# Growth and decay rows of the last tile of pass 1 loaded ahead, in buffers that nothing needs any more

## The reference

```python
q = (x @ Wq.T); k = (x @ Wk.T); v = (x @ Wv.T)            # [S, 16, 64] each
log_decay = -softplus(x @ Wd.T + bd)                      # [S, 16], one a head
k_gated = k * sigmoid(x @ Wg.T)
s_t = exp(g_t) * s_{t-1} + k_t^T v_t                      # state 64 x 64 a head
o_t = q_t s_t
out = rmsnorm(o) * norm_w * sigmoid(x @ Wog.T) @ Wo.T
```

## Time and profile before

| | us |
|---|---|
| three runs | 3225.49, 3229.1, 3230.01; median 3229.1 |
| profiled execution, its own time | 3229.59 |
| its span, first to last instruction | 3227.8 |
| TensorE busy | 3162.5 (98%) |
| VectorE, ScalarE, GpSimd busy | 1881.0, 1292.1, 470.6 |
| mean granted TensorE clock | 0.99 of full |

### The profile page before, as it was taken

One profiled execution on the slowest core, in us unless ns is written; L12 is line 12 of the kernel. 1 busy time (PEld: TensorE's weight loads), 2 busy tenths in 40 slices (PEclk: granted clock), 3 DMA queues, 4 the chain that ended last, 5 costly groups with the idle time before them and its releaser, 6 DMA issues. The chain is left out here.

```text
span 3227.8 us, 91060 instructions
## 1 busy us (share of the span) xinstructions
PE 3162.5 (98%) x37253; PEld 2968.2 (92%) x37253; DVE 1881.0 (58%) x4823; ACT 1292.1 (40%) x3584; POOL 470.6 (15%) x723
## 2 busy tenths in 40 slices
PE   7999999999999999999999979999999999999999
PEld 6999999999999999999999968999999999999998
DVE  5454554545554545555545455667666677767776
ACT  3444444444444444444444442333333333333332
POOL 0111111111111111111111112111111111111110
PEclk8999999999999999999999989999999999999999
DMA  6132222322222232222322243222222333332220
GB/s 216 59 104 73 96 86 69 106 68 97 84 79 96 69 99 81 87 89 71 103 75 92 77 149 95 78 78 78 78 79 82 83 84 81 81 81 79 78 78 27
DMA packets 273394, 279.46 MB, mean 87 GB/s; under 512 B 24720, under 2 KB 221344, under 8 KB 273072
## 3 DMA queue, kind: packets, MB, share of 16 engines
q1 hardware_dynamic: 270960, 270.67, 27.6%
q10 hardware_dynamic: 2112, 4.19, 0.4%
HBM read 189.84 MB, written 84.93 MB: 85 GB/s over the span
## 5 line engine op out<-in xcount | busy, mean ns | idle before, releaser
L55 PE MATMUL psJ<-h_hi,w_k_hi 128*128 128x256 f32 x1024 | 298.9, 292 | 0.0
L55 PE MATMUL psJ<-h_hi,w_q_hi 128*128 128x256 f32 x1024 | 296.2, 289 | 0.0
L55 PE MATMUL psJ<-h_hi,w_g_hi 128*128 128x256 f32 x1024 | 293.1, 286 | 2.7 <-DVE h_lo L883 2.1
L55 PE MATMUL psG<-h_hi,w_og_hi 128*128 128x256 f32 x1024 | 286.4, 280 | 4.1 <-PEq L348 4.1
L56 PE MATMUL psJ<-h_lo,w_q_hi 128*128 128x256 f32 x1024 | 286.6, 280 | 0.0
L56 PE MATMUL psJ<-h_lo,w_g_hi 128*128 128x256 f32 x1024 | 286.4, 280 | 0.0
L57 PE MATMUL psJ<-h_hi,w_g_lo 128*128 128x256 f32 x1024 | 286.4, 280 | 0.0
L57 PE MATMUL psJ<-h_hi,w_q_lo 128*128 128x256 f32 x1024 | 286.2, 279 | 0.2 <-issue 0.2
L56 PE MATMUL psJ<-h_lo,w_k_hi 128*128 128x256 f32 x1024 | 285.3, 279 | 0.0
L57 PE MATMUL psJ<-h_hi,w_k_lo 128*128 128x256 f32 x1024 | 285.3, 279 | 0.0
L56 PE MATMUL psG<-h_lo,w_og_hi 128*128 128x256 f32 x1024 | 283.6, 277 | 0.0
(11 more groups left out here) (264 smaller groups left out, 9404.5 us busy)
## 6 DMA issues: line engine op xcount, KB each, us to landing
grown<-cum_dram SPq DMA_DIRECT2D x256, 128.0 KB
cum_rows<-cum_dram SPq DMA_DIRECT2D x512, 64.0 KB, 3.9
o_dram<-o SPq DMA_DIRECT2D x256, 128.0 KB, 4.5
o_cols<-o_dram SPq DMA_DIRECT2D x128, 256.0 KB, 4.9
an_norm_x<-in_L_attn_x_dram SPq DMA_DIRECT2D x32, 512.0 KB, 3.7
h_dram<-h_hi SPq DMA_DIRECT2D x32, 512.0 KB, 3.6
h_dram<-h_lo SPq DMA_DIRECT2D x32, 512.0 KB, 4.6
h_hi<-h_dram SPq DMA_DIRECT2D x32, 512.0 KB, 3.9
```

The costliest lines, as they stand in the source:

```text
L55: nc.tensor.matmul(out, w_hi, x_hi, start=first, stop=False)
```

## The change

In all tiles: cum_rows now holds eight pairs (both halves of its places are used), with a semaphore for each pair, so decay rows no longer wait for the decays four pairs ahead; and at the end of a tile the growth rows of pairs 0 and 1 are issued first, then the decay rows.

At the end of tile 31 all eight pairs' decay rows are issued, not four. In the last tile the growth rows of pairs 2 and 3 go into gate, those of 4 and 5 into grown and those of 6 and 7 into the first two pairs of q, each once its place is dead; SyncE issues them ahead of and between the loads of jobs 0 and 1. And o of the last tile is made in kg, so copy_o waits for no store.

```diff
-        spread = [ctx.enter_context(nc.semaphore(f"a_spread{n}")) for n in range(4)]
+        spread = [ctx.enter_context(nc.semaphore(f"a_spread{n}")) for n in range(NP)]
+        grow_end = [ctx.enter_context(nc.semaphore(f"a_grow_end{n}")) for n in range(1, ND)]
+        grown_end = [grown, gate, grown, q[:, 0:2, :]]
...
-            return cum_rows[:, p % 4, 0:2, :]
+            return cum_rows[:, p % 4, p // 4 * 2:p // 4 * 2 + 2, :]
...
-            hold(sp, s["e"], NP * i + p - 3)
+            hold(sp, s["e"], NP * (i - 1) + p + 1)
...
+        def grow_rows_end(sp, i, d):
+            for e in range(2):
+                p = 2 * d + e
+                sp.dma_start(grown_end[d][:, e, :], cum_b[i, 1, 2 * p:2 * p + 2, :].unsqueeze(1).to_broadcast([2, DH, T])
+                             ).then_inc(grow_end[d - 1], 16)
+
+        def o_of(j, d):
+            if isinstance(j, int) and j == NT - 1:
+                return kg[:, 2 * d:2 * d + 2, :].rearrange("p e (h t) -> p e h t", h=NC)
+            return o
...
                 if not proj and d == 0:
+                    sp.wait_ge(s["k"], NP * NT)
+                    grow_rows_end(sp, j, 1)
                     sp.wait_ge(s["proj"], NU * NT)
                     sp.wait_ge(s["h_kept"], 32 * NT)
                     load_w(sp, 0)
+                    sp.wait_ge(s["qg"], NP * j + 2)
+                    grow_rows_end(sp, j, 2)
+                    sp.wait_ge(s["score"], ND * j + 1)
+                    grow_rows_end(sp, j, 3)
                     load_w(sp, 1)
...
-                if gla and d < 3:
+                if gla and proj and d < 3:
                     for p in (2 * d, 2 * d + 1):
                         grow_rows(sp, j, p + 2)
-                if gla and d < 2:
+                if gla and proj and d < 2:
                     for p in (2 * d, 2 * d + 1):
                         spread_rows(sp, j, p + 4)
...
                 for pair in range(2):
                     grow_rows(sp, i, pair)
-                    spread_rows(sp, i, pair)
-                for pair in range(2, 4):
+                for pair in range(4 if i < NT - 1 else NP):
                     spread_rows(sp, i, pair)
...
             for e in range(2):
-                hold(act, store[e], 16 * m)
-                nc.scalar.copy(o[:, e, :, :], psH[e]).then_inc(s["o_part"], 1)
+                if o_of(j, d) is o:
+                    hold(act, store[e], 16 * m)
+                nc.scalar.copy(o_of(j, d)[:, e, :, :], psH[e]).then_inc(s["o_part"], 1)
...
-                dve.wait_ge(grow[e], 16 * (ND * j + d + 1))
+                at_end = isinstance(j, int) and j == NT - 1 and d > 0
+                if at_end:
+                    dve.wait_ge(grow_end[d - 1], 32)
+                else:
+                    dve.wait_ge(grow[e], 16 * (ND * j + d + 1))
+                factor = grown_end[d] if at_end else grown
...
-            pool.wait_ge(spread[p % 4], 32 * (NP // 4 * i + p // 4 + 1))
+            pool.wait_ge(spread[p], 32 * (i + 1))
```

More of the change, by code:

```diff
@@ L440, in spread_rows @@
                              cum_b[i, 0, 2 * p:2 * p + 2, b * CH:(b + 1) * CH].unsqueeze(0).to_broadcast([DH, 2, CH])
-                             ).then_inc(spread[p % 4], 16)
+                             ).then_inc(spread[p], 16)
         def grow_rows(sp, i, p):
@@ L458, in store_o @@
             sp.wait_ge(s["o"], NP * j + p + 1)
-            sp.dma_start(o_v[j, :, p, :, :], o[:, p % 2, :, :]).then_inc(store[p % 2], 16)
+            sp.dma_start(o_v[j, :, p, :, :], o_of(j, p // 2)[:, p % 2, :, :]).then_inc(store[p % 2], 16)
         def sp_tile(sp, i, gla, proj, prep, opens=False):
@@ L899, in grow_q @@
                 dve.wait_ge(s["by_act"], act_done(j, ("q", p)))
-                dve.wait_ge(grow[e], 16 * (ND * j + d + 1))
+                at_end = isinstance(j, int) and j == NT - 1 and d > 0
[4 more added lines that the diff above has]
+                factor = grown_end[d] if at_end else grown
                 nc.vector.tensor_tensor(qg[:, e, :].rearrange("p (c b t) -> p c b t", b=2, c=NC),
-                                        q[:, p, :].rearrange("p (c b t) -> p c b t", b=2, c=NC), grown[:, e, :].rearrange(
-                    "p (b c t) -> p c b t", b=2, c=NC), ALU.mult).then_inc(s["qg"], 1)
+                                        q[:, p, :].rearrange("p (c b t) -> p c b t", b=2, c=NC),
+                                        factor[:, e, :].rearrange("p (b c t) -> p c b t", b=2, c=NC),
+                                        ALU.mult).then_inc(s["qg"], 1)
         def weigh_k(dve, j, d):
@@ L950, in sum_o @@
             for e in range(2):
-                nc.vector.tensor_tensor(o[:, e, :, :].rearrange("p h (b t) -> p h b t", b=2),
-                                        o[:, e, :, :].rearrange("p h (b t) -> p h b t", b=2),
-                                        psO[e].rearrange("p b (h t) -> p h b t", h=2), ALU.add).then_inc(s["o"], 1)
+                both = o_of(j, d)[:, e, :, :].rearrange("p h (b t) -> p h b t", b=2)
+                nc.vector.tensor_tensor(both, both, psO[e].rearrange("p b (h t) -> p h b t", h=2),
+                                        ALU.add).then_inc(s["o"], 1)
         def grow_state(dve, j, d):
```

## The result

The changed kernel takes 3244.93 us (median of 4 runs, 3241.54 to 3248.01), the kernel before beside it 3229.56 us: 0.5% slower, ratio 1.005 with a 95% interval of 1.0038 to 1.0062. Forecast were 3243.5 us and a range of 3231 to 3248. The profiled execution took 3248.01 us, 18.4 more than that of before.

What follows compares the result with a forecast made beforehand. In the last tile's four turns TensorE idles until VectorE is through. Load 1 landing late makes d = 1 end 16.2 us later, less 1.8 in d = 2: +14.4 on the median 3229.1 gives 3243.5 us, range 3231 to 3248.

Steps and rivals of the forecast that it cites:

- Full tiles: All tiles but the last: mask 0 ends 0.1 us late behind both growth rows, 0.84 us of cover hides it; 0.
- rival D: Full tiles with thinner cover: mask 0 costs TensorE up to 0.3 us a tile besides the forecast; 3247 to 3253, chance 0.04.
- End of tile 31: Eight more decay-row transfers add 5.1 us to SyncE's queue; d = 0 moves by +0.6 to -0.4, taken as 0.
- The line before two engines: Last tile, SyncE's queue: 2.7 to 2.9 us per growth-row transfer, about 2.75 per load; load 1 lands at 1910.1.
- What waits for load 1: GpSimd's scaling of job 1, mask 3, then ScalarE's decays of pair 3: d = 1 ends 16.2 us later.
- d = 2: Last tile's third turn: job 3's load finds its queue nearly empty, pair 5's mask comes sooner; 1.8 us back.
- d = 3: Last tile's fourth turn: growth rows long there before too, pair 7's mask waits for job 5 as before; 0.
- The waits that the change removed: Growth-row waits and ScalarE's 5.91 us store wait in d = 1 go, but lie under the wait for load 1; 0.
- Rival B: Growth rows form no line; load 1 is late only by its issue, landing 1894.4 to 1897.8; 3228 to 3231, chance 0.11.
- Rival C: Loads pass the growth rows on the fourteen other engines, load 1 usable by 1889.7 as before; 3225.9, chance 0.05.

Runs made afterwards that it cites:

- e1: Changed kernel, each growth-row transfer of the last tile sent as two halves of the form [64, 256], same queue places: 3238.41 us.
- e2: Changed kernel, load 1 issued right behind load 0, ahead of the growth rows of pairs 4 to 7: 3238.51 us.
- e8: Changed kernel, load 1 issued between the growth rows of pairs 4, 5 and those of 6, 7: 3238.88 us (one run).
- e3: Changed kernel, GpSimd masks pairs 3, 5 and 7 before it scales jobs 1, 3 and 5: 3239.91 us.
- e10: Kernel before, with only o of the last tile made in kg, so ScalarE's copies wait for no store: 3230.2 us.
- e9: Changed kernel, last-tile growth rows as halves, loads 0 to 2 ahead of later rows, masks before scaling, tile-end growth and decay rows in turn for four pairs: 3217.5 us.
- e6: Kernel before, with only GpSimd's order changed: masks 3, 5 and 7 ahead of scaling jobs 1, 3 and 5: 3224.96 us.

## Why the prediction was right

*Full tiles, 0 expected.* Right in size, but the reading behind it was too low. In the changed kernel ScalarE and TensorE waited from 100 to 1870 us (us in total, times, longest):

```profile
ACT prob L823 <- POOL cum_rows L1128: 5.4, 6, 1.7
```

```profile
PE psJ L55 <- ACT q L790: 0.9, 2, 0.6
```

ScalarE waited up to 1.7 us for a mask, where the tile of the earlier trace rows gave 0.1, and this is more than the 0.84 us of cover read there. So the sign given for rival D did show, but in six waits only, and at 0.9 us of TensorE's time.

*End of tile 31.* Sixteen decay-row issues took 10.95 us, not 10.2, and growth rows of d = 1 went out at mark 12.1 instead of 11.3. Mask 0 at mark 9.1 was forecast at 8.3.

*The line before two engines.* This step carries the forecast, and it is shown: by the 14.4 us between the landings of loads 0 and 1 in the changed kernel (the sum had 11.2 + 2.75 = 13.95), by e1 (another form, 8.9 us) and by the dose of e2 and e8. The issue of load 1 was far off: forecast at mark 15.1, it came at 26.0, as SyncE was held at its growth rows. The prediction had said that this would move only the waiting, and the gap between the landings bears it out. Load 1 was forecast at 35.9, it was usable at 37.8: 0.8 of the 1.9 us from the issues, 0.9 from growth rows that landed later behind them, 0.2 from the rest.

*What waits for load 1.* Decays of pair 3 end 18.0 us later by the mark (42.4 against 24.5; forecast 16.2, short by the 1.9 above, within 0.1). e3 shows that the mask is one of two ways by which load 1 holds d = 1; the prediction named the other, TensorE's turn of job 1, only as what comes behind.

*d = 2.* Forecast -1.8, measured -1.3: decays of pair 5 end at 55.8 against 39.1, 16.7 later. Job 3's load took 5.8 us instead of 6.99. The engines were free for it, as the forecast had it: the DMA view has 0 GB/s in all slices but one from 1916.5 to 1920.5. In e2, where they weren't, it took 10.0. *d = 3:* -0.1, and -0.2 behind it. The stage as a whole +16.4, forecast +14.4: the mechanism was right and its sum 2 us short.

*The waits that the change removed,* worth 0 where they stood: e10 shows it for the store wait, in the kernel before. For the growth rows of d = 1 nothing was removed, against the forecast: they landed at 20.9, as before, 1.7 us later than forecast.

Rival B (late only by its issue) is what e1 made of the kernel: load 1 lands 6.4 us behind its issue, within B's 5.1 to 8.5. Even that costs 9.4 us by the medians (3238.41 against 3229.01), not the -1 to +2 that B was given: the issue was put at mark 15.1 and came at 22.5, so the landing, put at 20.2 to 23.6, came at 28.9. B had SyncE's issues too cheap. Rival C fell with the landing itself. What the medians rose by, 15.4 us, is closer to the 14.4 than the stage's 16.4; with runs that scatter by 3 us that difference says nothing.

What stays open: what holds SyncE at its issues, why it needs 3.33 us for the first four halves of d = 1 in e1 and 2.43 for the next, and how much of e9's gain is each edit's; e6 alone gives 4.5 us of the 7.9 by which the stage is shorter.

## What to carry to other kernels

Price a transfer by its place in the line and by the engines that it uses, and not by its bytes alone: here 128 KiB on two engines held up what stood behind it for some 2.8 us, as long as the 1 MiB of a weight load. Look in the DMA view for stretches of low share and constant rate, and try another form for such a transfer as well as another place; here each alone took the changed kernel to 3238.4 and 3238.5 us. When a list of issues is reordered, follow each thing that moves back to all its consumers; here a weight load that seemed to be for later stood, through one engine's written order, before a mask that the current turn needed. And price each removed wait alone (e10: 5.91 us of wait, 0 gained), since another wait can end just behind it.

## What was not expected of the hardware

- SyncE's own issues stretched while loads and growth rows were queued before them: a pair of growth rows took 4.71 and 6.27 us to issue in the changed kernel, 1.09 at the empty queue.
- A load issued on ScalarE's queue wasn't apart from SyncE's line: 1 MiB took 5.8 us in the changed kernel with nothing else under way at its issue, and 10.0 us in e2 with SyncE's load 2, issued 1.7 us earlier, under way.
